# Three reorderings in a two-layer attention and expert kernel: when one norm, one add of gathered rows and four router scores are issued

## What is computed

```
x = x + L0_xattn(layernorm(x), ctx)   # cross attention, self attention, dense FFN; 16 heads of 16
x = x + L0_ffn(layernorm(x))          # 7 experts, top 2 of 8, 256 slots each: rows scattered, then gathered back
x = x + L1_xattn(layernorm(x), ctx)   # cross attention again: the "second layer"
x = x + L1_ffn(layernorm(x))          # scores = h @ w_router; the 128 rows with the top scores go through an FFN
```

## Time and profile before

| | |
|---|---|
| median of 3 runs | 878.05 us (877.8 to 879.11) |
| profiled execution, its own time | 874.34 us |
| span of that execution, first to last instruction | 872.6 us |
| mean granted TensorE clock | 0.92 of full speed |
| PE busy | 738.4 us (85%) |
| DVE busy | 647.7 us (74%) |
| ACT busy | 463.9 us (53%) |
| POOL busy | 406.7 us (47%) |

### The profile page before, as it was taken

How to read it: one execution, slowest core, us unless ns; L and a number is a source line. 1 busy time by engine, 2 the same in 40 slices (tenths; PEclk the granted TensorE clock), 3 DMA queues, 4 the chain that set the end, 5 groups by cost and what they waited for, 6 DMA issues and landing times.

```text
span 872.6 us, 18486 instructions
## 1 busy us (share of the span) xinstructions
PE 738.4 (85%) x7282; PEld 614.4 (70%) x7282; DVE 647.7 (74%) x1250; ACT 463.9 (53%) x739; POOL 406.7 (47%) x388
## 2 busy tenths in 40 slices
PE   5788999999999778999952899955688799689996
PEld 5656777777777448999852899954456576458996
DVE  7758888888888644898885477747878798836863
ACT  4256767777777576574511254412156567555451
POOL 7783655434654465537456241135763352622200
PEclk9889999999999899999985899986679899979998
DMA  6695786779685402001030677345768657200011
GB/s 186 129 149 98 142 125 92 111 118 141 97 123 106 61 2 98 25 2 44 19 111 17 219 247 231 132 84 97 118 107 112 85 79 99 29 2 1 30 33 37
DMA packets 57066, 81.49 MB, mean 93 GB/s; under 512 B 8434, under 2 KB 35057, under 8 KB 56932
## 3 DMA queue, kind: packets, MB, share of 16 engines
q1 hardware_dynamic: 53730, 74.11, 43.8%
q0 software_dynamic: 3072, 6.04, 2.9%
q10 hardware_dynamic: 178, 0.16, 0.1%
HBM read 36.74 MB, written 10.11 MB: 54 GB/s over the span
## 4 chain that ended last, share of the span: by engine, by line
PE 61%; DVE 17%; issue 6%; DMA 5%; POOL 5%; ACT 4%; SPq 2%; POOLq 0%; ACTq 0%; DVEq 0%
PE ps L214 12%; PE ps L216 10%; PE ps L215 10%; PE ps L761 7%; PE ps L829 7%; DVE nmax L1547 6%; PE ps L783 5%; PE ps L982 4%; POOL moe_in L1382 3%; DMA kst<-k_parts 2%; SPq L544 2%; ACT prob L1096 2%; PE ps L803 1%; PE ps L247 1%; POOL gat L1394 1%
## 5 line engine op out<-in xcount | busy, mean ns | idle before, releaser
L1547 DVE TENSOR_REDUCE nmax<-ps 128x4 f32<-128x1024 f32 x192 | 234.3, 1223 | 71.9 <-PE ps L761 70.5
L1096 ACT ACTIVATE prob<-ps 128x1024 f32<-128x1024 f32 x192 | 196.3, 1022 | 74.8 <-PE ps L783 72.7
L1305 POOL TENSOR_TENSOR rstd<-var,half 128x2 f32<-128x2 f32 x56 | 44.1, 788 | 256.4 <-DVE var L1474 184.0
L761 PE MATMUL ps<-kst,qst 50*128 50x256 f32 (+1 forms) x768 | 100.4, 341 | 35.7 <-DVE nmax L1547 27.8
L761 PEld LDWEIGHTS ps<-kst,qst 50*128 50x128 f32 (+1 forms) x768 | 61.4, 197 | 68.6 <-DVE nmax L1547 45.6
L829 PE MATMUL ps<-prob,vext 128*32 128x256 f32 x1536 | 108.5, 402 | 0.6 <-ACT oext L1109 0.6
L783 PE MATMUL ps<-qst,kst 51*128 51x256 f32 (+1 forms) x768 | 84.4, 299 | 14.0 <-ACT prob L1096 13.1
L783 PEld LDWEIGHTS ps<-qst,kst 51*128 51x128 f32 (+1 forms) x768 | 62.4, 197 | 21.3 <-ACT prob L1096 16.6
L829 PEld LDWEIGHTS ps<-prob,vext 128*32 128x32 f32 x1536 | 41.4, 112 | 33.2 <-issue 5.7
L1109 ACT ACTIVATE oext<-ps 128x256 f32<-128x256 f32 x96 | 36.9, 384 | 33.8 <-PE ps L829 17.9
L1313 POOL TENSOR_SCALAR hres<-xres,mv,rstd 128x256 f32<-128x256 f32 x42 | 51.8, 1241 | 2.2
(11 more groups left out here) (278 smaller groups left out, 2302.0 us busy)
## 6 DMA issues: line engine op xcount, KB each, us to landing
kst<-k_parts SPq DMA_DIRECT2D x138, 128.0 KB, 5.6
qst<-q_parts SPq DMA_DIRECT2D x132, 128.0 KB, 4.0
e_raw<-in_ein SPq DMA_DIRECT2D x7, 1024.0 KB, 5.2
e_raw<-in_eout SPq DMA_DIRECT2D x7, 1024.0 KB, 6.2
ctx_raw<-in_ctxT SPq DMA_DIRECT2D x16, 256.0 KB, 5.3
out<-xres SPq DMA_DIRECT2D x8, 256.0 KB, 2.1
moe_in<-zeros SPq DMA_DIRECT2D x14, 128.0 KB
moe_out<-vext SPq DMA_DIRECT2D x7, 256.0 KB, 5.7
```

The lines of the kernel that those rows point to most:

```text
L761: last = pe.matmul(score_pair(n, p)[:, 512 * s + S * t:512 * s + S * (t + 1)], qst[j][a:b, p, t * P:(t + 1) * P], kst[j][a:b, p, :], start ...
L1096: act.activation(probs[p % 4][:].rearrange("p i t s -> p (i t s)"), T_PS, ACT.Exp).then_inc(sm["exp_done"], 1)
L1305: last = gp.tensor_tensor(rstd[i][:], var[i][:], half[:], ALU.pow)
L1547: dve.tensor_reduce(nmax[n % 2][:, :, :, p].rearrange("p t s -> p s t"), score_pair(n, p).rearrange("p (s t k) -> p s t k", s=2, t=TB), AX ...
```

## The change

Three entries of the order tables change, and one wait is added. No instruction of work is added or removed.

```diff
         POOL_ORDER = {
...
-            "context 9.0": "context 8.0", "context 10.0": "attention 17.0", "gather 5.0": "gather 4.0", "attention 19.0": "gather 5.0",
-            "attention 16.1": "attention 19.0", "gather 7.0": "attention 18.1", "gather 6.0": "context 12.0",
+            "context 9.0": "context 8.0", "context 10.0": "attention 17.0", **behind("gather 4.0", "attention 19.0", "gather 5.0", "attention 16.1"),
+            "gather 7.0": "attention 18.1", "gather 6.0": "context 12.0",
         }
         DVE_ORDER = {
...
-            "combine 5.0": "attention 17.1", "combine 5.1": "combine 5.0", "queries 21.0": "attention 18.0", "attention 16.8": "attention 18.2",
+            "combine 5.0": "attention 17.4", "combine 5.1": "combine 5.0", "queries 21.0": "attention 18.0", "attention 16.8": "attention 18.2",
...
+            **behind("attention 23.7", "attention 16.13", "attention 17.13", "attention 18.13", "attention 19.13"),
         }
...
                         dve.wait_ge(sm["h_ready"], n + 1)
+                        if n > NA:
+                            dve.wait_ge(sm["score_s"], n - NA)
                         for t in range(TB):
                             last = dve.tensor_tensor_reduce(res[:, t, :], hb(n)[:, t, :], rows[:, R_SV + R_RT, :], 1.0, 0.0, ALU.mult, ALU.add,
```

## The result

The changed kernel took 882.76 us (median of 7 runs, 880.24 to 883.54), the kernel before beside it 878.05 us (870.73 to 879.11): a ratio of 1.0061, 95% interval 1.0031 to 1.0091. It is slower by 4.7 us in the medians, where the forecast was 2.0 us faster, 876.05. The profiled execution took 883.54 us, with a span of 881.8 us at a mean granted clock of 0.913; the one of before had 874.34, 872.6 and 0.92.

The account below looks back on a forecast made before the run. No engine was full; the prediction took PE's waits at 628 to 636 us and among the maxima up to 766 us as the bound. -2.2 - 0.3 + 0.5 = -2.0 us from 878.05 gave 876.05 us, range 873.0 to 879.2.

Parts of the forecast that it names:

- The norm between the gathers: On POOL, item 19's norm starts at 623.2, not 627.03; PE's 2.32 us wait goes; last gather issued at 631.0.
- With the same 6.64 us it lands at 637.6: Batch 5's last gather keeps its 6.64 us from issue to landing, so it lands 5.0 us later than before.
- Max 17.4 ends and the rows have landed, so the add does not wait: On DVE, max 17.4 ends at 638.7, after the 637.6 landing; batch 5's add starts unwaiting and takes 1.95 us.
- Max 17.2 -5.0, max 17.4 -2.3, max 17.6 -1.85: Earlier starts on DVE at the first place, in us; 2.2 was booked, bounds 1.0 and 3.7.
- walk at the full clock: First place recomputed at full clock: max 17.5 at 640.5, max 17.6 at 642.2, 3.7 us earlier.
- Passing it on: I take nothing off: From 645 to 767 us everything hangs on the same chain, so the first place's gain carries through undiminished.
- clock rival: Removed waits keep the clock full in 630 to 645 us, possibly the tail too: 873.75 us; chance 0.25.
- given back: The gain at max 17.2 is eaten by the landing or a later stage: -0.5 us, so 877.5; chance 0.15.
- Four scores leave the maxima: Removing scores of items 16 to 19 from DVE's maxima: item 16's gives 0.3 us, item 19's 1.2, the others 0.
- Four scores behind max 23.7: Scores take 3.0 us ahead of item 21's low half, 0.95 hidden, 2.05 not; PE waits.
- slower rival: In the tail, PE idles before item 21's projection and stays at low clock: 880.1 us; chance 0.15.
- The sum: Whole kernel: first place -2.2, item 16's score -0.3, scores behind max 23.7 net +0.5, together -2.0 us.

Follow-up runs that it names:

- full_small_k18: The changed kernel, but the six copies filling item 18's stack of keys bring 16 of 256 columns; median 872.8 us, ratio 0.9956.
- scores_only: The kernel before with only the four scores moved behind max 23.7, with their wait; median 876.9 us, ratio 1.0036.
- add_only: The kernel before with only batch 5's add moved from behind max 17.1 to behind max 17.4; median 877.4 us, ratio 1.0035.
- norm_only: The kernel before with only item 19's norm moved ahead of batch 5's gathers; median 879.5 us, ratio 1.0089.
- norm_add176: The kernel before with item 19's norm ahead of batch 5's gathers and batch 5's add behind max 17.6; median 875.3 us, ratio 1.0004.

## Why the prediction was wrong

- **The norm between the gathers: right.** The norm starts behind its variance, the last gather about 5 us later (636.36 less 5.6 us of shift is 630.7; 631.0 was said), PE's wait of 2.32 us is 0.29.
- **"With the same 6.64 us it lands at 637.6": this step failed.** It landed at 640.1 on the same scale, 9.41 us after its issue. The 6.64 us of the earlier trace rows was the time of a gather issued ahead of the keys' copies. I moved the gathers 5 us later on POOL's queue and did not look at what SP issues in those 5 us: six copies of 128 KB more stood ahead of the last gather, nine in place of three. I wrote that no other DMA changes its place; that was true, and it was the trap. full_small_k18 shows 4.7 us without the keys' copies.
- **"Max 17.4 ends and the rows have landed, so the add does not wait": fell with it.** It waited 1.71 us. The price of the add itself, 1.95, was 1.79.
- **Max 17.2 -5.0, max 17.4 -2.3, max 17.6 -1.85:** measured -5.2, -2.5 and -1.1. My lower bound for 17.6, 1.0, was for a landing 1 us late; it came 2.5 late and still gave 1.1. (In the walk at the full clock, 637.6, 1.95 and 1.2 add up to 640.75, and not to the 640.5 that I wrote; nothing hangs on it.)
- **"Passing it on: I take nothing off": the dearest error.** The 1.1 us at 17.6 were +4.0 at 18.7: the changed kernel idles 1.72 us at 649.92 and then has 0.53 of the clock in 650 to 661, where before had 1.00. I had booked the clock only as a possible gain. The wait and the fall behind it are worth 7.0 us (63.9 against 56.9). The clock rival's own sign did not come, 0.64 in 636 to 651 us, the same stretch, where it wanted over 0.8. Without the wait the place gives 3.0 us at 18.7, between its 3.7 and the forecast's 2.2.
- **The rival "given back"** named the late landing beside busy DMA engines and was the nearest to what happened, but it priced it as a gain lost, -0.5 us in all, and not as a loss.
- **Four scores leave the maxima: mis-sized.** -1.5 was said (0.3 for item 16's, 1.2 for item 19's), -2.7 measured up to max 23.7 (scores_only): 1.0 by max 20.7, the rest behind max 22.7.
- **Four scores behind max 23.7: mis-sized.** 3.0 us less 0.95 hidden was said. They took 3.63 us: about 0.2 us passed between two scores where I had 0.1, and one piece took 0.60 us and not 0.41. Less was hidden too: PE began the projection at 767.80 in the kernel before and not at the 768.1 that I had, so 0.66 us and not 0.95. PE's projection starts 3.03 us later than before (5.51 against 2.48 us behind max 23.7) and the residual 3.06, where 2.05 was said. PE waited 3.38 us, past the 3 that I had named as the sign of the slower case, since at the full clock it was also through with the transposed maxima sooner (they start 1.74 us behind max 23.7 and not 2.23).
- **The slower rival** had its mechanism in the tail: idle PE in front of the projection, and low clock behind. The idleness was there, but the tail's clock did not get worse (0.91 before, 0.93 after). Its time, 880.1, lies near the 882.76 for another reason: its place was the tail, and the larger loss was behind max 17.4. That 880.1 lies near is luck.
- **The sum:** said -2.2 - 0.3 + 0.5 = -2.0. Measured by segments of the profiles: +4.0 at 18.7, -1.9 up to 20.7, -1.5 up to 23.7, +2.9 in the tail, +3.5 in all. The ratios give +5.3 us (1.0061) and +3.6 us (1.0041), and both intervals hold it.

## What to carry to other kernels

When a transfer is moved later, its old time from issue to landing does not move with it: list what the other queues issue in the new stretch, first of all the large copies. Price an idle gap of PE not by its length but also by the clock behind it, and in both directions: here 1.7 us of waiting cost 7, while 1.6 us at the same place, in add_only, left the clock at the full level. Only a run tells which it is. Small work without a deadline belongs behind the last piece of work that the busy engine is about to wait for, not in front of it: the same four scores held PE up by 3.0 us on one side of item 21's low half and not at all on the other.

## What the runs showed that I had not expected

- The landing of an indirect gather of 128 rows went from 3.7 to 4.0 us beside no large copy to 9.4 us beside twelve copies of 128 KB.
- Making item 20's context load 16 times smaller changed the gathers' landing by nothing (9.45 against 9.44 us).
- The tail, in nearly one order of work, took 100.7 us at a clock of 1.00, 103.8 at 0.95 and 107.3 at 0.91. In repeated profiles of one kernel it was the same to 0.1 us, but what decides between these values stays open: norm_only and norm_add176 had the tail of before in their order and took 102 us, without the scores being moved.
- Two profiles of the kernel before agree to 0.1 us over the 265 us behind max 16.0 and differ by 4.5 us over the 600 us ahead of it.
